# Routing of the last expert layer: groups of eight tiles in place of four, and 24 shared tiles first

## The reference, cut to what matters

```python
x = x + attention(layernorm(x), ctx_1024, ctx_1024, q_w, k_w, v_w, o_w ...)   # L3, 16 heads of 8
...
xf = layernorm(x)                                     # what follows is L3_ffn
sg = einsum('td,sdh->tsh', xf, sw1); su = einsum('td,sdh->tsh', xf, sw3)
shared_out = einsum('tsh,shd->td', silu(sg) * su, sw2)         # for every token
logits = xf @ router_w.T + experts_bias                        # 8 experts
rw, sel = top_k(logits, 2); rw = softmax(rw)
moe_out = sum over the two chosen e of rw * ((silu(xf @ w1[e]) * (xf @ w3[e])) @ w2[e])
x = x + moe_out + shared_out
```

## Time and profile before

| | us |
|---|---|
| median of 3 runs (lowest, highest) | 1740.68 (1729.44, 1743.26) |
| the profiled execution, its own time | 1748.64 |
| its span, first to last instruction | 1746.9 |
| last attention, in the span | 1310 to 1538.7 |
| expert stage, first item to the last result | 1538.7 to 1721.7 |
| adding up and storing | 1721.7 to 1746.9 |

### The profile page before, as it was taken

One profiled execution on the slowest core, in us unless ns is written; L12 is line 12 of the kernel. 1 busy time (PEld: TensorE's weight loads), 2 busy tenths in 40 slices (PEclk: granted clock), 3 DMA queues, 4 the chain that ended last, 5 costly groups with the idle time before them and its releaser, 6 DMA issues. The chain is left out here.

```text
span 1746.9 us, 44346 instructions
## 1 busy us (share of the span) xinstructions
PE 1379.0 (79%) x16797; PEld 1150.8 (66%) x16821; DVE 1047.8 (60%) x2733; ACT 921.7 (53%) x2096; POOL 620.4 (36%) x604
## 2 busy tenths in 40 slices
PE   4799999977999997993588656877728878669993
PEld 3677777855788885872256535877625766559883
DVE  5676767755435326998799974333357778624334
ACT  2465656542444445986355334434466766316664
POOL 2322222320000002341478605676723245444542
PEclk9899999998999999996699969888968888679997
DMA  8200000009990002310000011111130000012224
GB/s 301 53 18 18 17 18 17 3 22 171 159 161 2 1 1 62 117 64 1 16 17 20 1 49 36 41 43 44 43 112 26 14 30 24 32 43 69 67 61 162
DMA packets 143515, 93.93 MB, mean 54 GB/s; under 512 B 55776, under 2 KB 130272, under 8 KB 142816
## 3 DMA queue, kind: packets, MB, share of 16 engines
q1 hardware_dynamic: 134368, 72.86, 19.3%
q0 software_dynamic: 8960, 18.50, 3.3%
HBM read 51.20 MB, written 40.12 MB: 52 GB/s over the span
## 5 line engine op out<-in xcount | busy, mean ns | idle before, releaser
L405 POOL TENSOR_TENSOR wide_probs<-wide_probs,wide_key_mask 128x512 f32<-128x512 f32 x64 | 82.9, 1316 | 197.7 <-ACT wide_probs L526 197.7
L1765 ACT ACTIVATE moe_hidden<-bank,moe_staged 128x128 f32<-128x128 f32 x288 | 82.6, 372 | 81.0 <-PE bank L1859 50.5
L1870 PE MATMUL bank<-moe_staged,moe_hidden 128*128 128x128 f32 x576 | 90.8, 308 | 41.9 <-ACT moe_hidden L1765 32.8
L1870 PEld LDWEIGHTS bank<-moe_staged,moe_hidden 128*128 128x128 f32 x576 | 81.3, 218 | 47.0 <-ACT moe_hidden L1765 36.7
L2601 DVE TENSOR_TENSOR moe_hidden<-bank,moe_gate 128x256 f32<-128x256 f32 x104 | 44.1, 424 | 103.6 <-ACT moe_gate L2687 79.5
L1541 POOL DMA_INDIRECT moe_x_rows<-moe_rows,moe_source x72 | 79.5, 1104 | 74.9 <-DVE moe_source L1637 53.3
L2591 POOL DMA_INDIRECT moe_results<-moe_y_rows,moe_x_rows x72 | 69.1, 960 | 92.2 <-DVE moe_y_rows L2613 68.2
L744 POOL MEMSET attn_v_bd<- 128x576 f32 x2 | 1.2, 618 | 269.3 <-POOLq L168 269.3
L774 POOL TENSOR_TENSOR attn_col_bd<-attn_col_t,group_mask_sb 128x1024 f32<-128x1024 f32 x32 | 60.9, 1902 | 90.6 <-ACT attn_row_t L975 90.6
L1547 POOL DMA_INDIRECT moe_results<-moe_y_rows,moe_dest x72 | 76.4, 1061 | 46.8 <-DVE moe_y_rows L1680 30.5
L1004 ACT ACTIVATE attn_probs<-attn_probs 128x1024 f32<-128x1024 f32 x64 | 64.2, 1051 | 49.7 <-DVE attn_probs L878 49.3
(11 more groups left out here) (416 smaller groups left out, 4262.9 us busy)
## 6 DMA issues: line engine op xcount, KB each, us to landing
moe_rows<-route_empty_sb SPq DMA_DIRECT2D x8, 2624.0 KB, 22.7
attn_ctx<-in_ctx_t SPq DMA_DIRECT2D x48, 128.0 KB, 2.1
moe_x_rows<-moe_rows SPq DMA_DIRECT2D x72, 66.0 KB
moe_pack_sb<-in_moe_pack SPq DMA_DIRECT2D x8, 578.0 KB, 4.0
moe_w_sb<-in_moe_w SPq DMA_DIRECT2D x2, 2048.0 KB, 9.9
moe_hot<-moe_results SPq DMA_DIRECT2D x16, 256.0 KB, 6.2
moe_y_in<-moe_results SPq DMA_DIRECT2D x16, 256.0 KB, 5.5
moe_pack_sb<-in_moe_pack SPq DMA_DIRECT2D x9, 384.0 KB, 4.4
```

What stands on the lines that cost most here:

```text
L405: nc.gpsimd.tensor_tensor(probs[b.parity][:, :, h2], probs[b.parity][:, :, h2], keys, ALU.mult).then_inc(masked, 1)
L1765: ins = nc.scalar.activation(hidden[m % 2][:, f], hid_bank[m % 2][:, f * P:(f + 1) * P], ACT.Gelu, bias=staged[b % STAGED][:, b1_at + f:b1 ...
L1870: ins = nc.tensor.matmul(y_bank[m % 2][:, 0:P], hidden[m % 2][:, f], weights[:, at:at + P], start=(f == 0), stop=(f == nf - 1))
```

## The change

`QUAD` becomes 8: four groups of eight tiles. Norm parts run in steps 7, 8, 11, 12, 15, 16, 19 and the tail; choosing in steps 11, 15, 19 and the tail; slots are placed in steps 12 and 16 and twice in the tail. Rows are made four tiles at a time (`make_rows`), in steps 8, 9, 12, 13, 16, 17 and twice in the tail. A send still takes four tiles: `piece` 0 to 3 of a group are k = 0 for its halves, then k = 1. They begin in step 12, one in each step; two pieces follow the steps, and six, 24 DMAs, fall into the expert stage (16 before). `SHARED_FIRST` becomes 24.

```diff
-QUAD = 4
+QUAD = 8
 QUADS = TILES // QUAD
+SENT = 4
...
-    def send(self, core, pool, g, k, after):
+    def send(self, core, pool, g, piece):
...
+        k, h = piece // 2, piece % 2
+        tiles = slice(QUAD * g + SENT * h, QUAD * g + SENT * h + SENT)
         pool.wait_ge(self.slotted, g + 1)
         if k == 1:
-            for t in range(QUAD):
-                pool.wait_ge(self.sent[t], after * DMA_INC)
+            for t in range(SENT):
+                pool.wait_ge(self.sent[SENT * h + t], (2 * g + 1) * DMA_INC)
...
+        rows_step = lambda n: 4 * (n // 2) + 8 + n % 2
+        rows_at = {rows_step(n): n for n in range(6)}
...
-                    if s >= 10:
-                        g, k = (s - 10) // 2, s % 2
-                        d.send(core, pool, g, k, 2 * g + 1)
-                d.send(core, pool, 5, 0, None)
-                d.send(core, pool, 5, 1, 11)
+                    if s >= 12:
+                        d.send(core, pool, (s - 12) // 4, s % 4)
+                for piece in range(2):
+                    d.send(core, pool, 2, piece)
...
-                    norming = (s - 5) // 2 if s % 2 == 1 else None
-                    spilled = (s - 6) // 2 if s % 2 == 0 else None
-                    choosing = (s - 9) // 2 if s % 2 == 1 else None
+                    norming = (s - 7) // 4 if s % 4 == 3 else None
+                    spilled = (s - 8) // 4 if s % 4 == 0 else None
+                    choosing = (s - 11) // 4 if s % 4 == 3 else None
+                    ranking = (s - 12) // 4 if s % 4 == 0 and s >= 12 else None
...
-                norm_parts(7, 7, NORM_PARTS)
-                dve.wait_ge(ranked, 6)
-                take_logits(12, 4, 24, True)
-                take_ranks(5, True)
-                place(5)
-                choose_parts(6, 0, CHOOSE_PARTS)
...
+                norm_parts(3, 7, NORM_PARTS)
+                take_ranks(2, False)
+                place(2)
+                take_logits(6, 2, small_bank(True), 0)
+                choose_parts(3, 0, CHOOSE_PARTS)
+                tally(3)
+                take_ranks(3, True)
+                place(3)
...
-                    if 0 <= s - 6 < 12:
-                        row(s - 6)
-                        take_rows(s - 6, s - 6, 1)
...
+                    if s in rows_at:
+                        make_rows(rows_at[s])
+                        take_rows(rows_at[s], pt_bank[1])
...
-SHARED_FIRST = 16
+SHARED_FIRST = 24
...
-                d.send(core, pool, 6, 0, None)
-                d.send(core, pool, 7, 0, None)
-                d.send(core, pool, 6, 1, 14)
-                d.send(core, pool, 7, 1, 14)
+                for piece in range(2, 8):
+                    d.send(core, pool, 2 + piece // 4, piece % 4)
```

117 lines of the change are left out of this document (46 added, 71 removed).

## The result

The changed kernel took 1751.8 us (median of 7, 1748.1 to 1753.8) where the kernel before, beside it, took 1738.9 (1729.4 to 1745.2): a ratio of 1.0075, 95% interval 1.0056 to 1.0094. The forecast was 1718.4 us with a range up to 1740. It is slower by 13 us where 22 us less were expected.

The account below looks back on a forecast made before the run. No engine was full: attention steps were a ring of waits lengthened by small VectorE instructions and sends, and expert items had gaps. Gains of 11.4 + 1.5 + 3.0 + 1.2 + 5.2 = 22.3 us from 1740.7 gave 1718.4, range 1698 to 1740.

Parts of the forecast that it names:

- steps 5 to 11: Attention: new steps priced as old ones of their kind, 70.8 us for 82.2, a gain of 11.4.
- step 16 to the last addition: Attention's end: step 17 loses norm and choice (6.5), gets 1.05 of rows, keeps a 2.5 us stall; gain 3.0.
- expert stage: Eight shared items leaving the mixed stretch save 8 x 1.1 us, longer sends cost 3.7; gain 5.2.
- Light steps: Attention steps without norm or choice take 7.8 us at a clock near 1.00; 5.1 to 6.5 us below heavy ones.
- Rivals 3 (the clock): Attention: TensorE's clock stays low, so light steps take 12.9 us each; 1745 us, or 1752; chance 0.07.
- 4 (heavy steps grow with width): Attention: norm and choice steps grow with group width and eat the light ones' gain; 1735 us; chance 0.06.
- the price of the sends: Attention: a send that meets a light step costs 2.5 us, from 11.59 - 9.12.
- costs nothing: Attention: the wait before a group's third and fourth piece is for sends two steps earlier, so it costs 0.
- 10 more us at 2.3 for 1.45 lose 3.7 us: Expert stage: 24 sends for 16 last 10 us more, with items at 2.3 us instead of 1.45; loss 3.7.
- The gaps of the mixed stretch: Expert stage: 19 gaps each close behind a shared item; moving eight shared items saves 1.1 us each, 8 x 1.1.
- Rival 2: Expert stage: shared items don't cause the gaps, so moving them brings nothing; 10 us gained, 1731 us; chance 0.22.
- Rival 1: Attention and expert stage: stalls go with the groups' choice, not the sends; 33.5 us gained, 1707 us; chance 0.15.

Follow-up runs that it names:

- before_first24_2: The kernel before with SHARED_FIRST = 24 instead of 16: ratio 0.9966 calm; the same kernel stalling, without the _2, 1748.4 us, ratio 1.0009.
- changed_again: The changed kernel as it is, timed again in the calm condition: 1673.6 us, ratio 0.9922 to the kernel before.
- landed_pieces: The changed kernel, but in the expert stage each four sends wait until the four before have landed: 1747.8 us, ratio 1.0003 to the kernel before, stalling.
- landed_eights: The changed kernel with a wait for landed sends only after each eight sends in the expert stage: ratio 0.9958 to the kernel before, calm.
- paced_and_landed: The changed kernel with sends of steps 17 to 19 waiting on TensorE's steps, plus the edit of landed_pieces: ratio 0.9996, repeated 0.9987, both calm.
- set 1: The first set of follow-up runs, four variants timed beside the kernel before, which took 1746.81 us: stalling.
- set 4: The first of three later sets meant to find the stalling condition again; the kernel before took 1688.52 us: calm.
- sets 2 and 3: Follow-up sets of variants of the changed kernel, set 3 also with it unedited; the kernel before took 1688.40 and 1687.95 us: calm.
- busy_no_sends: The changed kernel with 24 GpSimd tile settings in place of the expert stage's 24 sends, their rows left out: 1689.1 us, repeated (_2) 1694.5, calm.
- plain_dmas: The changed kernel with 24 plain SyncE transfers in place of the expert stage's 24 sends, their rows left out: 1669.7 us in one run, calm.
- both_kinds: The changed kernel with 32 shared tiles first and 48 plain SyncE transfers landing before the expert stage's 24 sends: 1690.3 us in one run, calm.
- the two repairs: Two edits to the changed kernel: sends of steps 17 to 19 wait on TensorE's steps (1747.6 us, ratio 1.0004, stalling), and that of landed_pieces.

## Why the prediction was wrong

Its terms against both conditions. Stalling: the earlier trace rows and the spans named in the earlier trace rows, less the windows of the profile after. Calm: before_first24_2 less changed_again, and for the shared tiles the ratio 0.9966.

```
us gained                          forecast   stalling   calm
steps 5 to 11                        11.4        9.3      8.0
steps 12 to 15                        1.5        2.9      2.0
step 16 to the last addition          3.0      -10.5     -1.4
tail                                  1.2        2.2      2.2
expert stage                          5.2      -13.6      4.3
  (of it 24 shared tiles first)       8.8        0        5.7
sum                                  22.3       -9.7     15.1
timed                                          -13.0     13.2
```

(The expert stage calm: 5.7 by the ratio, less the 1.4 us from 151.3 to 152.6 us, first to last item. The zero is the 1.0009 of before_first24. The sum of the stalling column is not the difference of the two profiled spans, 1746.9 and 1749.7 us: an expert stage further up, which the change doesn't touch, took 8.5 us less in the changed kernel's profile, 331.3 us from the last key spreading of the first attention layer to the first of the last, for 339.9.)

- **Light steps.** Right, in size and clock. Steps 5 and 6 came at 7.77 and 7.76, step 10 at 8.49, all at 1.00; steps 7 and 11 at 12.90 and 14.36. Rivals 3 (the clock) and 4 (heavy steps grow with width) are out. Rival 3's price, 1745 to 1752 us, is where the measurement fell, but by accident, since its mechanism is out. The 2.1 us missing of 11.4 lie in steps 8 and 9 (21.7 us for the 20.2 that they were given) and step 10 (0.7 over).
- **The step that failed: the price of the sends.** I priced a send by the step that it meets: "a send that meets a light step" costs 2.5 us, and for steps 16 on I wrote that step 17 "keeps a send stall of 2.5". I moved the pieces to new steps and never asked what now keeps them apart. Before, each four waited for slots of their own group, placed in every second step, for the key spreading, or, ahead of each copy L1915, for the k = 0 writes just issued to land. With groups of eight all four pieces of a group have their slots at once, and from step 17 on there is no key spreading in GpSimd's queue, and the k = 0 writes that the third piece needs are two pieces old: 16 sends ran in one row. That this wait "costs nothing" was true and looked at the wrong risk: the queue ran too fast, not too slow. In the stalling condition a row of four costs a stall of some 4 us at most; the row of 16 cost 10.5 us against before, 13.5 against the forecast, and the row of 24 20 us of waits.
- **The same mistake in the expert stage.** "10 more us at 2.3 for 1.45 lose 3.7 us" took the loss as proportional to the time of the sends. Before, they were two rows of eight with a pause behind the eighth (it ended at 1549.1 us, the ninth began at 1551.3) and waits of 2.70 and 3.46 us; one row of 24 is not three times a row of eight. landed_pieces shows it: 5.7 us of waits for 20.1 with the same 24.
- **The gaps of the mixed stretch** (8 x 1.1). Rival 2 was right as to mechanism. The count of gaps (16, 20) didn't follow the shared items, and calm there is one in changed_again and none in before_first24_2. That all 19 stood close behind a shared item misled. That the shared tiles yet bring 5.7 us when calm, near my 5.2, is then an accident of size: argued, not shown, it is that 16 items end before the first block can be read and turned, and 24 don't; the waits of 5.1 and 9.8 us in landed_eights and paced_and_landed are of that kind.
- **Rival 1** (the stall goes with the choice, not the sends) came out of the rule in the Trainium skill, SBUF — State Buffer, "Who interferes with whom": TensorE and ScalarE wait on nobody, and a DMA doesn't contend with a compute engine. Calm, the traces agree: TensorE works 35.7 of 37.6 us beside 24 sends. Stalling, they don't: ScalarE stands up to 13.6 us beside the same row, and nothing is chosen there. The stall of the earlier trace rows was of this second kind, and nothing in that profile said that the same kernel would run without it in other sets.

The forecast's sign is thus that of the calm condition, at 13 us of the 22. That is luck: it was made from a profile of the stalling one, priced stalls that the calm one doesn't have, and was wrong for the one that it was made for. Calm, too, the part from step 16 on gained nothing (-1.4 for 3.0, at a granted clock of 0.68 where before_first24_2 had 0.75); why is not shown.

**What the calm condition changes elsewhere.** The stages without indirect transfers are alike. The last key spreading of the first attention layer starts at 978.37 us in before_first24 and at 978.26 in before_first24_2, the same kernel in the two conditions. Behind it stands an expert stage, untouched by the change, in which GpSimd issues 144 indirect transfers. TensorE's groups there, stalling and calm:

```profile
L1870 PE MATMUL bank<-moe_staged,moe_hidden 128*128 128x128 f32 x576 | 87.8, 301 | 41.3 <-ACT moe_hidden L1765 32.5 <-issue 8.7
L1859 PE MATMUL bank<-moe_xb_t,moe_staged 128*128 128x128 f32 x576 | 86.9, 299 | 6.7 <-ACT moe_xb_t L1751 6.3
```

```profile
L1859 PE MATMUL bank<-moe_xb_t,moe_staged 128*128 128x128 f32 x576 | 78.3, 280 | 0.0
L1870 PE MATMUL bank<-moe_staged,moe_hidden 128*128 128x128 f32 x576 | 76.5, 276 | 0.3 <-ACT moe_hidden L1765 0.3
```

Waits of 48.0 us against 0.3, mostly on ScalarE. Not all of it is gained: calm, the same stage waits 46.5 us for gathered rows (L1844), stalling 7.9, which I take for GpSimd's own queue being the slowest there now; no run tests it. From that key spreading to the first one of the last attention there are 339.5 us stalling and 315.5 calm; in the last attention 220.0 and 210.1; from the first to the last item 183.7 and 151.3. That is 66.3 of the 67.7 us between the two spans, all of it in stretches in which GpSimd issues indirect transfers, though not all of it was traced to them.

**What stays open.** What makes a set stalling or calm. Theory D put it to the chip. The record numbers the chip: 0 in set 1 (stalling) and 0 again in set 4 (calm), 7 in sets 2 and 3, 14, 6 and 5 in those that followed. If the number means the same chip each time, which isn't on record, the chip alone doesn't decide, and something beside this kernel or in the state of the machine does. Slower packets are not what shows: those of the indirect transfers (q0 in the profile) fill 3.3% of 1749.7 us in the changed kernel's profile and 3.5% of 1670.9 us in changed_again, some 58 us for each DMA engine in both, and the larger queue of the kind that the profile calls "instruction" (q8) fills 0.5% in both. When a packet was asked for is not in the profile, so engines that wait for their own instructions stay a rival that nothing here excludes. Whether in the stalling condition the making of the transfers by GpSimd, their packets, or a busy GpSimd alone holds the others up: busy_no_sends, plain_dmas and both_kinds would tell, and never met it. And whether the two repairs add up there.

## What to carry to other kernels

When a change makes data ready in larger lots, look at what paced the queue that consumes it: the wait that vanishes may have been what spread its work out. Price a stall by the length of the row of transfers beside it, not by their number alone: pauses of 2 to 4 us after each four cut TensorE's waits here from 20 us to 6. Where nothing stalls the repairs cost: both together 11 us. And before explaining stalls beside indirect transfers, time both kernels in several sets: the same change was worth +13 and -13 us.

## What was not expected of the hardware

- Two conditions, 1687 to 1690 and 1739 to 1747 us for one kernel, each steady within a set, and apart, as far as the stages were compared, only in those with indirect transfers: beside the same row of 24 TensorE waits up to 11.1 us in the one, 0.6 in the other.
- A VectorE operation of 128 x 8 uint32 took 21.14 us, as long as GpSimd's 24 settings of a 128 x 1024 tile beside it (busy_no_sends_2). In the changed kernel VectorE meets only sends there and shows nothing like it:

```profile
1492.18 21.50 POOL L2573 MEMSET moe_idle<- 128x1024 f32 x24 [4.35 <-POOLq L168]
```

```profile
1492.56 21.14 DVE L2611 TENSOR_SCALAR moe_counts_u<-moe_counts_u 128x8 uint32<-128x8 uint32 x1
```

- Plain transfers of the same rows leave TensorE alone when calm even at 121 GB/s and a DMA share of 0.42 (both_kinds): 26.9 us of work in 27.3.
